# Masking the narrow diagonal tiles of a causal attention's maxima with TensorE instead of VectorE

## What is computed

```python
h = layernorm(x)
q, k, v = heads(h @ Wq), heads(h @ Wk), heads(h @ Wv)          # 16 heads of 16
scores = einsum('bhqd,bhkd->bhqk', q, k)
scores = where(tril(ones), scores, -inf)
x = x + merge(softmax(scores / sqrt(256)) @ v) @ Wo + bo
y = layernorm(x)
x = x + dequant(quant6(y)) @ dequant(quant6(weight)).T + bias
```

## Time and profile before

| | |
|---|---|
| median of 3 runs | 2134.79 us (2132.92 to 2139.34) |
| profiled execution | 2141.36 us, span 2139.6 us |
| mean granted TensorE clock | 0.981 |
| TensorE busy | 2022.3 us, 12037 matmul records |
| VectorE busy | 1738.0 us, 4442 instructions |
| ScalarE busy | 1361.8 us |
| GpSimd busy | 783.1 us |

### The profile page before, as it was taken

One profiled execution on the slowest core, in us unless ns is written; L12 is line 12 of the kernel. 1 busy time (PEld: TensorE's weight loads), 2 busy tenths in 40 slices (PEclk: granted clock), 3 DMA queues, 4 the chain that ended last, 5 costly groups with the idle time before them and its releaser, 6 DMA issues.

```text
span 2139.6 us, 36179 instructions
## 1 busy us (share of the span) xinstructions
PE 2022.3 (95%) x12037; PEld 794.5 (37%) x12037; DVE 1738.0 (81%) x4442; ACT 1361.8 (64%) x2905; POOL 783.1 (37%) x1099
## 2 busy tenths in 40 slices
PE   6799999999999999999999999999999999999994
PEld 3333333333333434343333344434333343333433
DVE  4797897877988787878888778796898998898865
ACT  5357666765766676667666666676666666777661
POOL 3323324231434454543234546363144443111232
PEclk9899999999999999999999999999999999999997
DMA  4441221313040322312213231231403112030000
GB/s 151 121 106 54 52 79 37 92 49 92 17 103 16 106 58 76 97 42 81 53 48 73 66 95 59 69 90 49 113 8 91 50 39 57 25 95 23 9 30 21
DMA packets 178327, 138.72 MB, mean 65 GB/s; under 512 B 54486, under 2 KB 178140, under 8 KB 178140
## 3 DMA queue, kind: packets, MB, share of 16 engines
q1 hardware_dynamic: 178140, 136.40, 23.3%
HBM read 85.20 MB, written 50.33 MB: 63 GB/s over the span
## 4 chain that ended last, share of the span: by engine, by line
PE 72%; DVE 17%; ACT 3%; issue 3%; SPq 2%; POOL 2%; DMA 1%; POOLq 0%; ACTq 0%; DVEq 0%
PE psum L1398 20%; PE psum L1381 19%; PE psum L1366 16%; DVE max_parts L1108 8%; PE psum L1464 8%; PE psum L1457 5%; DVE psum L1103 3%; ACT probs L911 2%; PE psum L1433 2%; SPq L633 1%; PE psum L1416 1%; ACT acc_sb L918 1%; PE psum L1486 1%; DVE max_parts L1103 1%; PE psum L1425 1%
## 5 line engine op out<-in xcount | busy, mean ns | idle before, releaser
L911 ACT ACTIVATE probs<-psum 128x512 f32<-128x512 f32 (+3 forms) x2560 | 1229.0, 538 | 682.5 <-PE psum L1381 673.8
L1108 DVE TENSOR_REDUCE max_parts<-psum 128x1 f32<-128x512 f32 x1536 | 971.1, 682 | 188.5 <-PE psum L1366 183.5
L1381 PE MATMUL psum<-q_rows,k_rows 99*128 99x512 bf16 (+3 forms) x2560 | 858.4, 352 | 5.1 <-ACT probs L911 3.4
L1366 PE MATMUL psum<-k_rows,q_rows 96*128 96x512 bf16 (+3 forms) x2560 | 819.4, 350 | 32.9 <-DVE max_parts L1108 10.1
L1398 PE MATMUL psum<-probs,v_in 128*17 128x512 f32 (+3 forms) x5120 | 596.7, 538 | 11.6 <-ACT acc_sb L918 10.2
L1103 DVE CUSTOM_DVE_ANT_0 psum<-psum,causal 128x128 f32<-128x128 f32 (+3 forms) x1024 | 477.0, 516 | 139.8 <-PE psum L1366 136.5
L1381 PEld LDWEIGHTS psum<-q_rows,k_rows 99*128 99x128 bf16 x2560 | 237.3, 98 | 642.1 <-ACT probs L911 496.7
L748 POOL TENSOR_SCALAR_AFFINE_SELECT probs<-probs 128x512 f32<-128x512 f32 x256 | 164.8, 644 | 803.0 <-ACT probs L911 802.6
L1366 PEld LDWEIGHTS psum<-k_rows,q_rows 96*128 96x128 bf16 x2560 | 245.0, 98 | 280.5 <-DVE max_parts L1108 57.1
L1398 PEld LDWEIGHTS psum<-probs,v_in 128*17 128x17 f32 x5120 | 86.2, 95 | 233.2 <-issue 166.5
L1103 DVE DVE_READ_ACCUMULATOR2_ANT max_parts<- 128x1 f32 x1024 | 143.5, 140 | 0.0
(11 more groups left out here) (158 smaller groups left out, 1359.3 us busy)
## 6 DMA issues: line engine op xcount, KB each, us to landing
q_rows<-qk_scratch SPq DMA_DIRECT2D x384, 64.0 KB, 2.6
k_rows<-qk_scratch SPq DMA_DIRECT2D x384, 64.0 KB, 2.7
qk_scratch<-shop SPq DMA_DIRECT2D x56, 384.0 KB, 2.9
shop<-in_L_attn_x SPq DMA_DIRECT2D x19, 512.0 KB, 4.1
v_scratch<-shop SPq DMA_DIRECT2D x16, 544.0 KB, 4.0
v_in<-v_scratch SPq DMA_DIRECT2D x64, 136.0 KB, 2.7
ctx_scratch<-ctx_out SPq DMA_DIRECT2D x60, 128.0 KB, 1.7
out_shop<-in_L_attn_x SPq DMA_DIRECT2D x12, 512.0 KB, 5.4
```

The source lines that it names most:

```text
L911: nc.scalar.activation(probs[s % NPROBS][:, h, a:CHUNK], bank[SCORE_BANKS[n % 3]][:, a:CHUNK], ACT.Exp, scale=SCALE).then_inc(probs_ready, 1)
L1108: nc.vector.tensor_reduce(max_parts[k % 2][:, first:first + heads, t % TILES, c], ring_bank(UNIT_USE[n])[:, 0:heads * width] .rearrange("p ...
L1366: ins = nc.tensor.matmul(dst[:, i * width:(i + 1) * width], q_rows[u][0:ROWS, qc, first + i, t % TILES * P:(t % TILES + 1) * P], k_rows[u] ...
L1381: nc.tensor.matmul(bank[SCORE_BANKS[n % 3]][:, a:CHUNK], k_rows[u][0:ROWS + LEVELS, h, kb * P:(kb + 1) * P], q_rows[u][0:ROWS + LEVELS, qc ...
```

## The change

Of the diagonal units, those with several heads in a bank (widths 128 and 256) are masked by TensorE: behind each head's matmul a second one adds the identity times a triangle of -1e38, `maskb`, into the last 128 columns of the head's region. VectorE then takes one plain maximum over the whole bank, with one result for each head, as for tiles off the diagonal. The units with one head (widths 384 and 512) keep the custom operation. GpSimd makes the new constant at the start.

```diff
+def masked_by_vector(n):
+
+    k, t, c, first, heads = UNITS[n]
+    return c == QCS[k] and heads == 1
...
+        maskb = sbuf("maskb", [P], BF16)
...
             nc.gpsimd.memset(ident[:, :], 0.0)
+            nc.gpsimd.memset(maskb[:, :], 0.0)
...
+            nc.gpsimd.affine_select(out=maskb[:, :], in_=maskb[:, :], compare_op=ALU.is_ge, fill=MASKED, base=0,
+                                    pattern=[[-1, P]], channel_multiplier=1)
             nc.gpsimd.affine_select(out=triangle, in_=triangle, compare_op=ALU.is_ge, fill=MASKED, base=0,
                                     pattern=[[-1, P]], channel_multiplier=1).then_inc(consts_ready, 1)
...
                 dve.wait_ge(unit_ready, n + 1)
-                if c == QCS[k]:
-                    if n == 0:
-                        dve.wait_ge(consts_ready, 1)
-                    for i in range(heads):
-                        mine = ring_bank(UNIT_USE[n])[:, i * width:(i + 1) * width]
-                        ins = nc.vector.tensor_tensor_reduce(
-                            out=mine, in0=mine, in1=causal[:, CHUNK - width:CHUNK], scale=1.0, scalar=LOWEST, op0=ALU.add, op1=ALU.max,
-                            accum_out=max_parts[k % 2][:, first + i, t % TILES, c:c + 1])
-                    ins.then_inc(unit_used, 1)
+                if masked_by_vector(n):
+                    dve.wait_ge(consts_ready, 1)
+                    mine = ring_bank(UNIT_USE[n])[:, 0:width]
+                    nc.vector.tensor_tensor_reduce(
+                        out=mine, in0=mine, in1=causal[:, CHUNK - width:CHUNK], scale=1.0, scalar=LOWEST, op0=ALU.add,
+                        op1=ALU.max, accum_out=max_parts[k % 2][:, first, t % TILES, c:c + 1]).then_inc(unit_used, 1)
                     return
                 nc.vector.tensor_reduce(max_parts[k % 2][:, first:first + heads, t % TILES, c],
                                         ring_bank(UNIT_USE[n])[:, 0:heads * width]
...
                                            k_rows[u][0:ROWS, first + i, c * CHUNK:c * CHUNK + width],
-                                           start=True, stop=True)
+                                           start=True, stop=c < qc or masked_by_vector(n))
+                    if c == qc and not masked_by_vector(n):
+                        ins = nc.tensor.matmul(dst[:, (i + 1) * width - P:(i + 1) * width], identb[:, :], maskb[:, :],
+                                               start=False, stop=True)
                 ins.then_inc(unit_ready, 1)
```

## The result

Over 15 executions of each, the changed kernel takes 2142.98 us (2139.97 to 2147.33) and the kernel before 2136.76 us (2130.91 to 2141.79). The ratio is 1.0028, with a 95% interval from 1.0019 to 1.0037: +6.0 us, 4 to 8. The forecast was +14.3 us and slower by more than 0.3%. The sign was right and the size more than twice too large. The prediction put what can be told from no change at about 0.3%, and 0.28% lies just under it.

What follows compares the result with a forecast made beforehand. TensorE was taken to pace the kernel, VectorE only in short stretches. Masks +21.0 less VectorE's saving 6.7 gave +14.3 us on 2134.8: 2149.1 us, own range 2142 to 2156 (0.50); 2131 to 2165 at 8 in 10.

Steps and rivals of the forecast that it cites:

- Count and price of the masks: On TensorE: 512 more matmuls of 128 columns at 0.057 us each, 29.2 us.
- rivals with exposed weight loads or a waiting accumulation: On TensorE's masks: exposed loads, 79 us as upper bound; accumulation waiting, +83 us over the 29, 2247 at most, chance 0.04.
- VectorE's operations: On VectorE: 64 and 128 plain maxima with four and two outputs near 0.68 us each, 512 masked ones left.
- about 110: Sign on VectorE: its busy time was to go down by about 110 us.
- 39 us by starts: VectorE's saving, from distances between starts: 25.9 us on four-head units and 13.4 us on two-head units.
- The waits for VectorE: TensorE's true wait for VectorE's maxima before units: between 13.1 and 74.6 us, roughly 44 us; VectorE's saving takes under a sixth.
- The chain's sign: In the chain of work that ended last: TensorE's share rises, VectorE's falls by less than two points.
- I charge the masks with TensorE's share of the chain: TensorE's masks, 29.2 x 0.72 = 21.0 us; VectorE's saving likewise by its share, 39.3 x 0.17 = 6.7 us.
- at 9 tenths or more: Reading of TensorE's granted clock: at 9 tenths or more, its 2.4 GHz level, nearly everywhere; no term charged.
- The work is hidden: Rival: masks fall under TensorE's waits for ScalarE and later ones for VectorE; 0 to +8 us, 2135 to 2143, chance 0.14.
- Faster: Rival: VectorE paces the pass of maxima; for example -8.5 us, 2126 us; chance 0.12.
- x = 0.43: Break-even: x is the part of changed units where the chain runs over VectorE; above 0.43 the change pays; shares make 0.19.

Runs made afterwards that it cites:

- the later plan: Transposes of attention's output planned two slots later (ready = load + 4, not load + 2); on the kernel before alone, ratio 0.9968, -6.8 us.
- e12: Kernel before plus TensorE's masks only, VectorE masking as before, transposes of attention's output two slots later; 1.0050 of the kernel before, +10.7 us.
- e13: Changed kernel without TensorE's masks, plain maxima only, transposes of attention's output two slots later; 0.9933 of the kernel before, -14.3 us.
- e9: Kernel before with the transposes of attention's output planned two slots later (ready = load + 4); 0.9968 of the kernel before, -6.8 us.
- e11: Changed kernel with no mask at all in the pass of maxima, transposes of attention's output two slots later; 0.9933 of the kernel before, -14.3 us.
- e10: Changed kernel with the transposes of attention's output planned two slots later; 1.0040 of the kernel before, +8.5 us.
- e6: Second measurement of the kernel before plus TensorE's masks only, VectorE masking as before; 1.0098 of the kernel before, +20.9 us.

## Why the prediction was off

- **Count and price of the masks: right.** 512 records, 0.06 us apart, 26.8 us over the narrow slots, where 29.2 was forecast. (The prediction misread one row on the way: TensorE's slices stand at 9 in all but the first two and the last, not the first three. Nothing hangs on it.) The rivals with exposed weight loads or a waiting accumulation were rightly given little, and the 81 ns per matmul that the Trainium skill ("TensorE: Matmul & The Clock Gate", "Back-to-back issue gap") gives at 128 columns do not hold for this stream: the starts in the timeline above are 60 ns apart.
- **VectorE's operations: right.** 683 to 691 ns for plain maxima. Its busy time fell by 40 us and not by "about 110": the sum of the rows' durations counts reads that run beside the next maximum, as the prediction itself said when it took 39 us by starts and then forgot in its list of signs.
- **The waits for VectorE: right in size.** Ahead of a unit's weight load, idle time that the maxima ended fell from 57.1 + 17.5 to 55.5 + 9.4 us, and ahead of its matmul from 13.1 to 9.0; the mean of the two falls by 7 us. The chain's sign failed: VectorE's share was to fall by less than two points and fell by seven. The matmul's rows:

```profile
  DVE max_parts L1115: 8.3, 24
...
  DVE max_parts L1111: 0.7, 3
```

- **"I charge the masks with TensorE's share of the chain", 21.0 us, and VectorE with its own, 6.7 us: the step that failed.** The masks alone cost 17 us (13 and 21 in two measurements), and VectorE's saving alone is worth 10.9 us (7 to 15), 7.5 with the later plan. Each term is off by 4 us in its middle, and both the same way, so +14.3 became +6. A chain's share tells how much of an engine's work was on the path, on average; it does not say what the delay meets next. The masks' delay met, among many short waits, one long one in each batch, for a transfer that takes 5.5 to 6.1 us from its first issue to the transposes in both profiles, and fell into it. The list of waits showed no such thing as large, since there are only three of this kind, 6.4 us in all; one had to look for the longest, not for the largest sum.
- **What was missing: the clock.** The prediction read the clock's slices as "at 9 tenths or more" and let it go. Those few tenths were 7 us at the batch starts of the first profile, and an edit that changes when TensorE gets there can change them. As estimated from the starts in the traces (each matmul's distance to the next, against the usual shortest for the two shapes), 28 us were added from first to last scores, the waits fell by 16 us, and the time lost to the lower clock by 10, of which 5 are the luck near the end. By the averages of the clock it was 5 to 6.
- **The rivals.** "The work is hidden" was right in kind, with its upper end at +8 us; it named ScalarE's waits and VectorE's, which gave a part, and not the transfer's. That 2142.98 us also lies in the forecast's own range of 2142 to 2156 is luck: the kernel before took 2136.8 us in the 15 executions, 2 us more than in the three on which the range was set. "Faster" had its break-even at x = 0.43; no run puts x there.
- **What is left open:** how the 16 us that the waits gave back divide among single waits, why the masks alone cost no more with the later plan, and the sum of e12 and e13. Why the clock fell at a wait of 1.52 us at the third batch start before, and held through one of 1.71 us in the changed kernel, isn't explained by any run here.

**The better version.** Of versions that compute the true maximum, e9 is the fastest, 0.32% below the kernel before, with one number changed. With a bound in place of the maximum, e11 and e13 are 0.67% below. In both pairs that were run (before and changed, e9 and e10) TensorE's masks cost more than they save on VectorE.

## What to carry to other kernels

Work added to the engine that paces this kernel showed up nearly in full where it was added, and still was not the cost: ask what the delay runs into within the next slots, and look for the longest single waits on transfers, not only at the sums by line. Before moving work, take such a wait out first; here that gained 7 us by itself, and with it the change's price was 15 us and not 6. A saving on the second engine counts where it has a queue, not where it sits idle in front of the work that was made shorter: two thirds of VectorE's saving brought an eighth of the gain, with an error as large as a third. And look at the clock of many executions before reading a difference from one pair of profiles: this pair's 0.981 and 0.988 were the ends of their kernels' spreads.

## What the hardware showed

The granted clock fell to its lower level behind a standstill of 2.5 us in the midst of a stream that was otherwise without gaps, and the matmuls behind it took up to 1.8 times as long (1.97 against 1.09 us for eight transposes). The windows of the kernel before around it, with length and busy time of TensorE, the granted clock, and share and rate of DMA:

```profile
506.30:509.70 3.40, 3.40 (x23) 1.00 0.63 152
509.70:513.10 3.40, 1.50 (x13) 1.00 0.76 193
513.10:516.50 3.40, 2.76 (x11) 0.50 1.05 239
516.50:519.90 3.40, 3.40 (x13) 0.50 0.72 165
519.90:523.30 3.40, 3.13 (x19) 1.00 0.00 0
```

This wait of 2.5 us so cost about 5.6 by estimate: itself, and half of the 6.2 us that TensorE worked at the lower level (6.8 us less the last 0.6 of the wait). Other waits cost only themselves: 1.82 us in e6, and even 3.21 us near the end of the changed kernel. The other surprise is how cheap a 128-column mask is: 0.06 us with its own weights and onto the result of the matmul before it, a quarter of the 0.22 us from one matmul of 512 columns to the next.
